# Repairs of the signal's ends in three sets of 4, 12 and 16 samples a layer, in place of eight of 4, in a four-layer convolution kernel

## The chip, the cores and the metric

The kernel runs on one core of one Trainium2 chip. Its engines are TensorE (PE; its weight load is listed apart as PEld), VectorE (DVE), ScalarE (ACT), GpSimd (POOL) and SyncE (SP), which issues most transfers. The metric is the device time of one execution in microseconds, lower is better. A profile is one execution, and its span runs from the first to the last instruction.

## The reference

The input `x` is 32 samples x 64 channels x 1024 positions. Four layers follow each other; each computes `x = x + ffn(cond(x, style))`, where `cond` is a chain of four modulated convolutions and `ffn` a layer of 1024 x 1024 with low-rank additions (another kind in each layer):

```python
TYPES = ('same', 'upsample', 'same', 'downsample')

def _layer(x, style, w, b, mw, mb, typ):
    s = style @ mw.T + mb
    weight = SCALE * w * s[:, None, :, None]
    demod = lax.rsqrt(jnp.sum(weight * weight, axis=(2, 3)) + EPS)
    weight = weight * demod[:, :, None, None]
...
x = x + _L0_ffn_ref(_L0_cond_ref(x, cond_512, ...), L0_ffn_A, L0_ffn_B, L0_ffn_Wr, L0_ffn_br)
x = x + _L1_ffn_ref(_L1_cond_ref(x, cond_512, ...), L1_ffn_gate, L1_ffn_kernel, ...)
x = x + _L2_ffn_ref(_L2_cond_ref(x, cond_512, ...), L2_ffn_base_W, L2_ffn_gate_W, ...)
x = x + _L3_ffn_ref(_L3_cond_ref(x, cond_512, ...), L3_ffn_W, L3_ffn_b, L3_ffn_A, ...)
```

The kernel composes the last three convolutions into one filter per sample. That composition is right inside the signal, but not at its first and last positions, where each single convolution pads with zeros. So the ends are computed again by the four convolutions one after the other, on the 8 positions at each side.

## The kernel before

**Steps.** Samples are worked on in 16 pairs per layer. A step is one pair; two steps (j = 0, the even one, and j = 1, the odd one) make one pass of a hardware loop `Fori` over `i`, and each engine runs its own such loop. Step n of a layer transposes and projects pair n, convolves pair n + 1 and prepares pair n + 2: `halves` and `filter` compose its filter, `first` applies the first convolution. Engines meet at semaphores only. `drain`, `enter` and `fill` are straight code between the loops of two layers; they also prepare the next layer's weights and modulations (`mods`), and end that with `mods_ready`.

**The repair of the ends.** It has five stages. Stage 0 (VectorE) scales the loaded ends into `e_x`. Stages 1 to 4 are one convolution each: three matmuls (six in stage 4) of plain fp32 on TensorE (`pe_edge`, L1055 and L1046), whose result VectorE scales, shifts and writes to `e_h`, `e_z`, a second tile that the profile also calls `e_z`, and `e_y` (`dve_edge`, L782 to L801). `end_hi` and `end_lo` take two values that `dve_first` copies into the convolution's input (L739, L740), and `dve_y` copies `e_y` into the result (L755). A set is four samples, so a layer has eight sets. Set 0 is repaired in `enter`, and set i + 1 in the even step of pass i, with the stages laid between the other matmuls of that step. TensorE waits for a stage where a bank of PSUM is used again:

```python
            if edges:

                pe.wait_ge(s["dve_e"], edge_count(l, i + 1, 4))
            if more:
                pe_halves(pe, l, n + 2)
            if edges:
                pe_edge(pe, l, i + 1, 2)
```

**The filter.** ScalarE and VectorE write a pair's filter to `filt`, and SyncE then shifts parts of it to other partitions by four transfers (L321, L322); the convolution (`pe_conv`) waits for them. In the odd steps of layer 0 SyncE also loads a block of the layer 1 kernel (`load_kernel`) ahead of the shift.

**Loads of the ends.** GpSimd issues them (`pool_load_edge`, L300 and L308). The tile `e_in` holds one set, and the next set is asked for when stage 0 has read it.

## Time and profile before

| what | before |
|---|---|
| median of 3 runs | 1951.31 us (1949.11 to 1953.24) |
| span of the profiled execution | 1944.8 us |
| TensorE busy | 1829.3 us, 94% |
| its weight loads | 1520.9 us, 78% |
| VectorE busy | 874.8 us, 45% |
| ScalarE busy | 667.7 us, 34% |
| GpSimd busy | 96.2 us, 5% |
| mean granted clock of TensorE | 0.966 |

The profile has no device time of its own execution, only the span, so the span stands beside the runs: it is 4.3 to 8.4 us below them. TensorE's busy time counts matmuls; weight loads run beside them.

### The profile page before, as it was taken

The page shows a single profiled execution, that of the slowest core. Times are in us where ns is not written, and L with a number is a line of the kernel's source. Part 1 is how long each engine was busy: PE and PEld are TensorE (multiplying, and loading weights), DVE is VectorE, ACT ScalarE, POOL GpSimd, SP SyncE. Part 2 cuts the span into 40 slices and gives each one's busy share as a digit, 9 for nine tenths or more (in the row PEclk, how much of TensorE's full clock was granted, in tenths as well). Part 3 has the DMA queues.
Part 4 walks back from the last instruction along what each step waited for, and adds up shares of the span by engine and source line. Part 5 has one row for each costly group of instructions (what it writes and reads, how often), then busy time and mean ns, then how long its engine had stood idle before and what let it go on. Part 6 is the DMA issues. An engine that isn't in the chain of part 4 may idle for free.

```text
span 1944.8 us, 28665 instructions
## 1 busy us (share of the span) xinstructions
PE 1829.3 (94%) x9728; PEld 1520.9 (78%) x9728; DVE 874.8 (45%) x2573; ACT 667.7 (34%) x1237; POOL 96.2 (5%) x173
## 2 busy tenths in 40 slices
PE   5889998979999999999899999999989999999995
PEld 4777787767888888887788888888767888888873
DVE  5155555644333333455543444444563333333327
ACT  2355555433333323325333222332253323332310
POOL 2000000010000000010000000000100000010000
PEclk9889999969999999999999999999999999999996
DMA  6565666436323322325322222221242222222218
GB/s 121 126 147 143 149 151 162 108 93 95 81 70 86 79 67 74 78 67 129 88 70 73 59 67 62 74 73 42 68 114 54 73 62 74 80 77 62 63 43 324
DMA packets 229831, 181.27 MB, mean 93 GB/s; under 512 B 178648, under 2 KB 189944, under 8 KB 229534
## 3 DMA queue, kind: packets, MB, share of 16 engines
q1 hardware_dynamic: 222142, 173.35, 34.7%
q10 hardware_dynamic: 2640, 5.26, 0.9%
q0 software_dynamic: 5008, 2.14, 0.9%
q8 instruction: 23, 0.38, 0.1%
q14 instruction: 18, 0.15, 0.0%
HBM read 108.34 MB, written 42.99 MB: 78 GB/s over the span
## 4 chain that ended last, share of the span: by engine, by line
PE 78%; issue 9%; DVE 4%; SPq 3%; DMA 3%; ACT 2%; POOL 0%; POOLq 0%; DVEq 0%; ACTq 0%
PE ps L970 64%; PE ps L1784 4%; PE ps L1055 3%; SPq L1321 3%; PE ps L1103 2%; DMA filt<-filt 2%; PE ps L1046 1%; ACT w_hi L1448 1%; PE ps L1804 1%; DVE x_last L1939 0%; POOL limes_rep L1864 0%; DVE filt L745 0%; DMA raw<-in_x 0%; PE ps L1996 0%; DMA raw<-in_L_ffn_base_W 0%
## 5 line engine op out<-in xcount | busy, mean ns | idle before, releaser
L970 PE MATMUL ps<-xp_hi,filt 128*128 128x512 f32 x1024 | 332.3, 406 | 13.5 <-DMA filt<-filt 12.0
L970 PE MATMUL ps<-w_hi,y_hi 128*128 128x512 f32 x768 | 314.1, 409 | 0.0
L970 PE MATMUL ps<-w_hi,y_lo 128*128 128x512 f32 x768 | 306.7, 399 | 0.0
L970 PE MATMUL ps<-w_lo,y_hi 128*128 128x512 f32 x768 | 305.8, 398 | 0.0
L970 PEld LDWEIGHTS ps<-xp_hi,filt 128*128 128x128 f32 x1024 | 187.2, 190 | 54.4 <-DMA filt<-filt 13.7
L734 DVE SCALAR_TENSOR_TENSOR xp_lo<-ps,mods_pair,xp_hi 128x512 fp32r<-128x512 f32 x128 | 96.2, 752 | 289.2 <-ACT xp_hi L403 289.1
L403 ACT ACTIVATE xp_hi<-ps,mods_pair 128x512 fp32r<-128x512 f32 x128 | 88.3, 690 | 379.9 <-PE ps L970 379.9
L970 PE MATMUL ps<-xp_lo,filt 128*128 128x512 f32 x512 | 202.5, 396 | 0.0
L970 PEld LDWEIGHTS ps<-w_lo,y_hi 128*128 128x128 f32 x768 | 146.2, 190 | 35.7
L419 ACT ACTIVATE y_nat<-ps,mods_pair 128x512 f32<-128x512 f32 x128 | 99.6, 778 | 215.3 <-PE ps L970 215.3
L970 PEld LDWEIGHTS ps<-w_hi,y_hi 128*128 128x128 f32 x768 | 147.3, 192 | 31.7
L970 PEld LDWEIGHTS ps<-w_hi,y_lo 128*128 128x128 f32 x768 | 146.6, 191 | 30.9
L428 ACT ACTIVATE y_hi<-ps 128x512 fp32r<-128x512 f32 x96 | 55.9, 599 | 324.2 <-PE ps L1103 324.2
L830 DVE TENSOR_TENSOR x_res<-ps,x_res 128x1024 f32<-128x1024 f32 x48 | 58.6, 1221 | 187.7 <-PE ps L970 187.7
L970 PE MATMUL ps<-x_hi,first_hi 128*128 128x512 f32 x256 | 109.3, 427 | 7.8 <-DVE w_lo L1452 5.9
L970 PEld LDWEIGHTS ps<-xp_lo,filt 128*128 128x128 f32 x512 | 97.4, 190 | 22.8
L755 DVE COPY y_nat<-e_y 128x4 f32<-128x4 f32 x128 | 21.8, 170 | 197.3 <-ACT y_nat L419 196.7
L308 POOL DMA_DIRECT2D e_in<-x_state x96 | 58.5, 616 | 1034.7 <-DVE e_x L782 994.5
L970 PE MATMUL ps<-x_lo,first_hi 128*128 128x512 f32 x256 | 104.3, 407 | 0.0
L970 PE MATMUL ps<-x_hi,first_lo 128*128 128x512 f32 x256 | 104.0, 406 | 0.0
L970 PE MATMUL ps<-fb_hi,up_hi 128*128 128x256 f32 x320 | 91.9, 287 | 0.0
L970 PE MATMUL ps<-fb_lo,up_hi 128*128 128x256 f32 x320 | 91.3, 285 | 0.0
(313 smaller groups left out, 3096.9 us busy)
## 6 DMA issues: line engine op xcount, KB each, us to landing
x_in<-x_state SPq DMA_DIRECT2D x96, 256.0 KB, 3.8
x_res<-x_state SPq DMA_DIRECT2D x48, 512.0 KB, 4.0
x_state<-x_res SPq DMA_DIRECT2D x46, 512.0 KB, 2.9
filt<-filt SPq DMA_DIRECT2D x128, 128.0 KB, 2.7
filt<-filt SPq DMA_DIRECT2D x128, 96.0 KB, 2.4
raw<-in_x SPq DMA_DIRECT2D x16, 512.0 KB, 4.9
x_res<-in_x SPq DMA_DIRECT2D x16, 512.0 KB, 4.0
x_state<-raw SPq DMA_DIRECT2D x16, 512.0 KB, 3.5
```

The source lines that it names most:

```text
L308: gp.dma_start(e_in[:, h, :, side, :], xs_edge[g, h, :, :, side * (M - 4):side * (M - 4) + 4]).then_inc(s["e_loaded"], 16)
L403: nc.scalar.activation(xp_hi[:, q, 1:M + 1], ps[:, 3 + 2 * q, :], ACT.Identity, bias=mods_pair[:, par, BX, q:q + 1]).then_inc(s["act_p"], 1)
L419: nc.scalar.activation(y_nat[q][:], ps[:, 6 + q, :], ACT.Identity, bias=mods_pair[:, par, CB, q:q + 1], scale=mods_pair[:, par, DS, q:q + ...
L428: nc.scalar.activation(y_hi[:, :, C * q:C * q + C], src, ACT.Copy).then_inc(s["act_t"], 1)
L734: nc.vector.scalar_tensor_tensor(xp_lo[:, q, 1:M + 1], ps[:, 3 + 2 * q, :], mods_pair[:, par, BX, q:q + 1], f(xp_hi[:, q, 1:M + 1]), ALU.a ...
L755: nc.vector.tensor_copy(ends, e_y[:, 2 * par + q]).then_inc(s["dve_y"], 1)
L830: nc.vector.tensor_tensor(dst.rearrange("p (h m) -> p h m", h=2), ps[:, 0:2, :], res, ALU.add).then_inc(s["dve_o"], 1)
L970: ins = nc.tensor.matmul(out, st[x0], mv[x1], start=first and t == 0, stop=last and t == 2, **kw)
L1055: last = mm(ps[0:rows, bank, 0:8 * width].rearrange("p (b e w) -> p b e w", b=4, e=2), st[k], rhs, start=k == 0, stop=k == 2)
L1103: last = nc.tensor.transpose(ps[:, 3 + 2 * q, P * t:P * t + P], y_nat[q][:, P * t:P * t + P], ident[:])
L1321: act.dma_start(dst, src).then_inc(s["small_loaded"], 16)
L1784: last = nc.tensor.matmul(ps[:, 0 if l == 0 else 6, 0:PROJ_W[l]], y_f[:, kb], proj[:, kb, 0:PROJ_W[l]], start=kb == 0, stop=kb == KB - 1)
```

## The change

The samples of a layer are repaired in three sets, which `EDGE_GROUPS` lists as first sample and count: 0 and 4, 4 and 12, 16 and 16. The first is still repaired on the way into the layer, the second in the even step of pass 0, the third in that of pass 3. These two passes are written out ahead of the loops over passes 1 to 2 and 4 to 6, on TensorE and VectorE only. Tiles of the repair hold 16 samples; `end_hi`, `end_lo` and `e_y` hold all 32, and are indexed by a register in the loops. The large tiles share memory with weights of the preparation, so their zero columns are written anew in each layer (four memsets ahead of `mods_ready`), and loads of the second and third set wait for `mods_ready`. The first set has a tile of its own, `e_first`. The diff, cut to its core:

```diff
 WIN = 4
 EDGE_OPS = 10
+EDGE_GROUPS = ((0, 4), (4, 12), (16, 16))
+EDGE_SETS = len(EDGE_GROUPS)
+EDGE_MOST = 16
+EDGE_STEPS = {0: 1, 3: 2}
...
         fb_hi, fb_lo = (sb(f"fb_{r}", [P, 2, WIN, C], F32R) for r in ("hi", "lo"))
+        with ExitStack() as area:
+
+            e_all = sb("e_all", [C, 2, EDGE_MOST, 2, 4], stack=area)
+            e_x = sb("e_x", [C, EDGE_MOST, 18], stack=area)
+            e_h = sb("e_h", [C, EDGE_MOST, 16], stack=area)
+            e_z = sb("e_z", [P, EDGE_MOST, 14], stack=area)
+            e_z2 = sb("e_z2", [P, EDGE_MOST, 12], stack=area)
...
-        e_y = sb("e_y", [P, 4, 2, 2])
+        e_first = sb("e_first", [C, 2, EDGE_GROUPS[0][1], 2, 4])
+        e_y = sb("e_y", [P, B, 2, 2])
+
+        def e_in(g):
+
+            return (e_first if g == 0 else e_all)[:, :, 0:EDGE_GROUPS[g][1]]
+
+        def e_in_nat(g):
+
+            n = EDGE_GROUPS[g][1]
+            t = (e_first if g == 0 else e_all)[:].rearrange("p a b e m -> p (a b e m)")
+            return t[:, 0:16 * n].rearrange("p (b e w) -> p b e w", b=n, e=2)
...
+            return EDGE_OPS * (EDGE_SETS * l + g) + step
+
+        def edge_set(k):
+
+            return sum(2 * k >= first for first, _ in EDGE_GROUPS) - 1
+
+        def edge_stage(l, g, stage_no):
+
+            return 4 * (EDGE_SETS * l + g) + stage_no
...
         def pool_load_edge(gp, l, g):
 
-            if not (l == 0 and is_zero(g)):
+            first, count = EDGE_GROUPS[g]
+            if g > 0:
+
+                gp.wait_ge(s["mods_ready"], l + 1)
+            if not (l == 0 and g == 0):
 
                 gp.wait_ge(s["dve_e"], edge_count(l, g - 1, 2))
             if l == 0:
                 for side in range(2):
-                    gp.dma_start(e_in_nat[:, :, side, :],
-                                 x_edge[g, :, :, side * (L - 8):side * (L - 8) + 8]).then_inc(s["e_loaded"], 16)
+                    gp.dma_start(e_in_nat(g)[:, :, side, :],
+                                 x_edge[:, first:first + count, side * (L - 8):side * (L - 8) + 8]).then_inc(s["e_loaded"], 16)
                 return
             for q in range(2):
 
-                gp.wait_ge(stored[q], 16 * (GROUPS * (l - 1) + g + 2))
+                gp.wait_ge(stored[q], 16 * (GROUPS * (l - 1) + (first + count) // 4 + 1))
             for h in range(2):
                 for side in range(2):
-                    gp.dma_start(e_in[:, h, :, side, :],
-                                 xs_edge[g, h, :, :, side * (M - 4):side * (M - 4) + 4]).then_inc(s["e_loaded"], 16)
+                    gp.dma_start(e_in(g)[:, h, :, side, :],
+                                 xs_edge[h, :, first:first + count, side * (M - 4):side * (M - 4) + 4]).then_inc(s["e_loaded"], 16)
...
+            for t, pad in ((e_x, 17), (e_h, 15), (e_z, 13), (e_z2, 11)):
+                v.memset(t[:, :, 0:pad + 1:pad], 0.0)
             v.memset(f(x_hi[:, :, 0:1]), 0.0)
             v.memset(f(x_lo[:, :, 0:1]), 0.0).then_inc(s["mods_ready"], 1)
...
-            b = 2 * par + q
-            nc.vector.tensor_copy(xp_hi[0:C, q, 1:M + 2:M], f(end_hi[:, b]))
-            nc.vector.tensor_copy(xp_lo[0:C, q, 1:M + 2:M], f(end_lo[:, b])).then_inc(s["dve_p"], 1)
+            b = ds(2 * k + q, 1)
+            nc.vector.tensor_copy(xp_hi[0:C, q:q + 1, 1:M + 2:M], f(end_hi[:, b]))
+            nc.vector.tensor_copy(xp_lo[0:C, q:q + 1, 1:M + 2:M], f(end_lo[:, b])).then_inc(s["dve_p"], 1)
...
-            nc.vector.tensor_copy(ends, e_y[:, 2 * par + q]).then_inc(s["dve_y"], 1)
+            nc.vector.tensor_copy(ends.unsqueeze(1), e_y[:, ds(2 * k + q, 1)]).then_inc(s["dve_y"], 1)
 
         def dve_edge(dve, l, g, stage_no):
 
             v = nc.vector
+            b0, n = EDGE_GROUPS[g]
 
             def mod(m, rows, width):
-                return mods[rows, m, ds(4 * g, 4)].unsqueeze(2).to_broadcast([rows.stop - rows.start, 4, width])
...
+                1: (2, lo_r, 14, e_h[:, 0:n, 1:15], G1, BT1),
+                2: (4, all_r, 12, e_z[:, 0:n, 1:13], G2, None),
+                3: (7, all_r, 10, e_z2[:, 0:n, 1:11], G3, BT3),
+                4: (7, all_r, 4, e_y[:, b0:b0 + n].rearrange("p b e m -> p b (e m)"), DS, None)}[stage_no]
+            dve.wait_ge(s["pe_e"], edge_stage(l, g, stage_no))
+            src = ps[rows, bank, 0:n * src_w].rearrange("p (b w) -> p b w", w=src_w)
             first = 2 * stage_no + 1
             done(v.tensor_tensor(dst, src, mod(mul, rows, src_w), ALU.mult), first)
             if stage_no == 1:
 
...
+        def dve_step(dve, l, i, j, more, one_more, g_next=None, g_y=None):
             n = 2 * i + j
-            edges = more and j == 0
-            g_y = i if j == 0 else i + 1
+            edges = g_next is not None
             if more:
                 dve_mods_pair(dve, l, n + 2, j)
             if edges:
-                dve_edge(dve, l, i + 1, 0)
+                dve_edge(dve, l, g_next, 0)
             if l > 0:
                 dve_y_lower(dve, l, n)
             if more:
...
         def pe_edge(pe, l, g, stage_no):
             mm = nc.tensor.matmul
 
+            n = EDGE_GROUPS[g][1]
             pe.wait_ge(s["dve_e"], edge_count(l, g, 2 * stage_no))
             if stage_no == 4:
                 for h in range(2):
                     for k in range(TAPS):
-                        rhs = e_z2[:].rearrange("p b (e w) -> p b e w", e=2)[:, :, :, k + h:k + h + 3:2]
-                        last = mm(ps[C * h:C * h + C, 7, 0:16].rearrange("p (b e w) -> p b e w", b=4, e=2),
+                        rhs = e_z2[:, 0:n].rearrange("p b (e w) -> p b e w", e=2)[:, :, :, k + h:k + h + 3:2]
+                        last = mm(ps[C * h:C * h + C, 7, 0:4 * n].rearrange("p (b e w) -> p b e w", b=n, e=2),
                                   down_T[:, k], rhs, start=k == 0, stop=k == 2)
...
-        def pe_step_0(pe, i, j, more, one_more):
+        def pe_step_0(pe, i, j, more, one_more, g_next):
             l, n = 0, 2 * i + j
-            edges = more and j == 0
+            edges = g_next is not None
             pe_transpose_y(pe, l, n, one_more)
             if one_more:
                 pe_conv(pe, l, n + 1, 0)
             if edges:
-                pe_edge(pe, l, i + 1, 1)
+                pe_edge(pe, l, g_next, 1)
 
             pe.wait_ge(s["act_f"], whole_y(l, n, 1))
...
-            for t in (e_x, e_h, e_z, e_z2):
-                gp.memset(t[:], 0.0)
             for t in (up_hi, up_lo, end_hi, end_lo):
                 gp.memset(f(t[:]), 0.0)
...
                 if l + 1 < LAYERS:
                     load_cond_weights(gp, l + 1)
-                with gp.Fori(0, GROUPS - 1) as i:
-                    pool_load_edge(gp, l, i + 1)
+                for g in range(1, EDGE_SETS):
...
-                with dve.Fori(0, GROUPS - 1) as i:
+                for i0, i1 in ((0, 3), (3, GROUPS - 1)):
                     for j in range(2):
-                        dve_step(dve, l, i, j, True, True)
+                        dve_step(dve, l, i0, j, True, True, EDGE_STEPS[i0] if j == 0 else None, edge_set(2 * i0 + j + 1))
+                    with dve.Fori(i0 + 1, i1) as i:
+                        for j in range(2):
+                            dve_step(dve, l, i, j, True, True, None, EDGE_STEPS[i0])
                 if l + 1 < LAYERS:
                     dve_drain(dve, l)
                 else:
...
-                with pe.Fori(0, GROUPS - 1) as i:
+                for i0, i1 in ((0, 3), (3, GROUPS - 1)):
                     for j in range(2):
-                        pe_step(pe, l, i, j, True, True)
+                        pe_step(pe, l, i0, j, True, True, EDGE_STEPS[i0] if j == 0 else None)
+                    with pe.Fori(i0 + 1, i1) as i:
+                        for j in range(2):
+                            pe_step(pe, l, i, j, True, True)
```

What stands where changes as follows, at the places that matter most. First TensorE in an even step of layer 1, in the loop, between the convolutions of the pair's two samples (`filt0`, `filt1`). Before:

```order
L970 MATMUL ps<-xp_hi,filt0 128x512 x2
L970 MATMUL ps<-xp_lo,filt0 128x512
L1041 ISA
L1055 MATMUL ps<-e_x,first_T 128x56 x3
L970 MATMUL ps<-xp_hi,filt1 128x512 x2
L970 MATMUL ps<-xp_lo,filt1 128x512
```

After, in the loop over passes 1 to 2 of that layer:

```order
L1000 MATMUL ps<-xp_hi,filt0 128x512 x2
L1000 MATMUL ps<-xp_lo,filt0 128x512
L1000 MATMUL ps<-xp_hi,filt1 128x512 x2
L1000 MATMUL ps<-xp_lo,filt1 128x512
L1000 MATMUL ps<-xp_hi,filt1 128x512 x2
```

Stage 1 and its wait (ISA) have left the looped steps, and so have the other stages. In the written-out even step of pass 3 they stand with sixteen samples, with 224 columns for 56:

```order
L1000 MATMUL ps<-xp_hi,filt0 128x512 x2
L1000 MATMUL ps<-xp_lo,filt0 128x512
L1086 MATMUL ps<-e_x,first_T 128x224 x3
L1000 MATMUL ps<-xp_hi,filt1 128x512 x2
L1000 MATMUL ps<-xp_lo,filt1 128x512
```

Second, VectorE at the end of a layer's preparation, where the last modulations are made. Before:

```order
L696 TENSOR_TENSOR mods<-ps,mods 128x32
L697 TENSOR_SCALAR mods<-mods,bias_col 128x32
L699 MEMSET x_hi 128x2
L700 MEMSET x_lo 128x2
L709 COPY mods_pair<-mods 128x20
```

After:

```order
L724 TENSOR_TENSOR mods<-ps,mods 128x32
L725 TENSOR_SCALAR mods<-mods,bias_col 128x32
L728 MEMSET e_x 64x16x2
L728 MEMSET e_h 64x16x2
L728 MEMSET e_z 128x16x2
L728 MEMSET e_z2 128x16x2
L729 MEMSET x_hi 128x2
L730 MEMSET x_lo 128x2
L739 COPY mods_pair<-mods 128x20
```

Four memsets have come in between the modulations and the last memset, which signals `mods_ready`.

## Rows read from the trace of the kernel before

**Rows 1.** The page: span, and busy time of each engine.

```profile
span 1944.8 us, 28665 instructions
...
PE 1829.3 (94%) x9728; PEld 1520.9 (78%) x9728; DVE 874.8 (45%) x2573; ACT 667.7 (34%) x1237; POOL 96.2 (5%) x173
```

**Rows 2.** Windows, odd then even step, layers 1 to 3: start:end length, busy (records), clock.

```profile
530.51:557.22 26.71, 26.71 (x137) 22.43 (x136) 9.06 (x22) 8.73 (x17) 0.00 (x0) 1.00 0.34 86
557.22:587.20 29.98, 29.98 (x168) 25.11 (x167) 12.54 (x37) 9.94 (x19) 2.45 (x4) 1.00 0.26 68
1031.11:1060.35 29.24, 29.24 (x153) 24.66 (x151) 12.17 (x38) 9.44 (x18) 0.00 (x0) 1.00 0.27 69
1060.35:1092.86 32.51, 32.51 (x183) 27.36 (x182) 14.51 (x51) 8.27 (x17) 2.43 (x4) 1.00 0.24 63
1491.83:1517.96 26.13, 26.13 (x134) 21.53 (x133) 9.16 (x23) 8.58 (x16) 0.00 (x0) 1.00 0.29 78
1517.96:1547.35 29.39, 29.39 (x163) 24.19 (x162) 11.42 (x36) 8.58 (x16) 2.44 (x4) 1.00 0.27 70
```

**Rows 3.** Windows of layer 0: five pairs of steps, and one odd step.

```profile
143.59:331.71 188.12, 175.87 (x1032) 146.52 (x1031) 107.80 (x315) 99.42 (x186) 6.12 (x10) 1.00 0.63 149
240.29:256.58 16.29, 15.77 (x89) 13.42 (x89) 9.65 (x25) 10.56 (x19) 0.00 (x0) 1.00 0.59 151
```

**Rows 4.** Waits of TensorE in those five pairs: us in total, times, longest.

```profile
PE ps L970 <- DMA filt<-filt: 9.6, 5, 2.4
PE ps L970 <- DVE zt_lo L1767: 2.6, 5, 0.5
```

**Rows 5.** Groups by line and shape, TensorE's fp32 matmuls: records, busy us, mean ns.

```profile
L1784 PE MATMUL ps<-proj,y_f 128*128 128x136 f32 x256 | 35.0, 292 | 0.7 <-ACT y_f L430 0.7
...
L1055 PE MATMUL ps<-e_x,first_T 64*128 64x56 f32 x192 | 29.8, 291 | 6.5 <-DVE e_x L777 5.2 <-DVE e_x L782 1.3
L1055 PE MATMUL ps<-e_h,up_st 64*128 64x48 f32 x192 | 29.0, 286 | 0.0
...
L1055 PE MATMUL ps<-e_z,mid_T 128*128 128x40 f32 x192 | 25.6, 276 | 0.0
...
L1046 PE MATMUL ps<-e_z,down_T 128*64 128x16 f32 x384 | 21.7, 214 | 0.0
```

**Rows 6.** Timeline of an even step of layer 0: start us, us, engine.

```profile
226.66 0.21 DVE L797 TENSOR_TENSOR e_h<-e_h,mods 64x56 f32<-64x56 f32 x1
...
227.29 0.75 DVE L728 SCALAR_TENSOR_TENSOR x_lo<-raw,mods_pair,x_hi 128x512 fp32r<-128x512 f32 x1
...
227.59 0.43 PE L970 MATMUL ps<-gu_hi,mid_hi 128*128 128x384 f32 x1
```

**Rows 7.** The way from layer 0 to 1: timeline, and TensorE's wait there.

```profile
401.29 0.06 DVE L699 MEMSET x_hi<- 128x2 f32 x1
...
PE ps L1055 <- DVE e_x L782: 1.3, 1, 1.3
```

**Rows 8.** First step of layer 2: its window, and TensorE's waits in it.

```profile
935.84:969.37 33.53, 32.79 (x181) 27.39 (x182) 14.41 (x53) 9.82 (x19) 2.43 (x4) 1.00 0.27 76
...
PE ps L1103 <- DVE xp_lo L740: 1.3, 2, 0.7
```

**Rows 9.** The shift in layer 0: timeline and transfer, even step; the chain, odd step.

```profile
236.56 0.63 SPq L322 DMA_DIRECT2D filt<-filt  x1
...
filt<-filt SPq DMA_DIRECT2D x1, 128.0 KB, 2.7
...
240.28 0.85 PEld L1103 LDWEIGHTS ps<-ident,y_nat 128*128 128x128 f32 x8 [0.44 <-DVE e_y L801]
...
253.77 5.60 DMA filt<-filt
```

**Rows 10.** The page, transfers of instructions: queue, packets, MB, share of 16 engines.

```profile
q8 instruction: 23, 0.38, 0.1%
```

**Rows 11.** Window of another even step of layer 3; the last numbers are clock, DMA, GB/s.

```profile
1629.01:1659.95 30.94, 30.94 (x163) 25.35 (x163) 11.43 (x36) 8.57 (x16) 2.44 (x4) 0.94 0.26 66
```

More of the change, by code:

```diff
@@ L156, in build @@
         xp_lo = sb("xp_lo", [P, 2, M + 4], F32R)
-        end_f = sb("end_f", [C, 4])
-        end_hi, end_lo = (sb(f"end_{r}", [C, 4, 2], F32R) for r in ("hi", "lo"))
+        end_f = sb("end_f", [C, EDGE_MOST])
+        end_hi, end_lo = (sb(f"end_{r}", [C, B, 2], F32R) for r in ("hi", "lo"))
         filt = [sb(f"filt{q}", [P, WIN, 2, 2, C], F32R) for q in range(2)]
@@ L780, in dve_edge @@
                 for h in range(2):
[L781 to L782 removed]
+                    dst = e_x[:, 0:n, 1:17].rearrange("p b (e m h) -> p b e m h", e=2, h=2)[:, :, :, :, h]
+                    done(v.tensor_tensor(dst, e_in(g)[:, h], m, ALU.mult), h + 1, False)
                 return
             bank, rows, src_w, dst, mul, add = {
[L785 to L790 removed]
+                1: (2, lo_r, 14, e_h[:, 0:n, 1:15], G1, BT1),
[4 more added lines that the diff above has]
+            src = ps[rows, bank, 0:n * src_w].rearrange("p (b w) -> p b w", w=src_w)
             first = 2 * stage_no + 1
@@ L798, in dve_edge @@
             elif stage_no == 2:
-                done(v.tensor_tensor(dst, dst, up_bias[:, ds(4 * g, 4), :], ALU.add), first + 1)
+                done(v.tensor_tensor(dst, dst, up_bias[:, b0:b0 + n, :], ALU.add), first + 1)
             else:
@@ L1142, in pe_step_0, with pe_step @@
             if edges:
-                pe_edge(pe, l, i + 1, 4)
+                pe_edge(pe, l, g_next, 4)
             pe_tail(pe, l, i, j)
             if edges:
-                pe.wait_ge(s["dve_e"], edge_count(l, i + 1, EDGE_OPS))
-        def pe_step(pe, l, i, j, more, one_more):
+                pe.wait_ge(s["dve_e"], edge_count(l, g_next, EDGE_OPS))
+        def pe_step(pe, l, i, j, more, one_more, g_next=None):
             if l == 0:
-                pe_step_0(pe, i, j, more, one_more)
+                pe_step_0(pe, i, j, more, one_more, g_next)
                 return
             n = 2 * i + j
-            edges = more and j == 0
+            edges = g_next is not None
             pe_transpose_y(pe, l, n, one_more)
```

86 lines of the change are left out of this document (36 added, 50 removed).

## The prediction

> **What bounds the kernel now.** I read the profile's page first. TensorE is busy for 1829.3 of the 1944.8 us span, every other engine for less than half (PEld is its own weight load) [rows 1]. What counts is therefore TensorE's own work, and the few places where it waits. Then I cut the trace into steps. A step begins with the transposes of `y_nat` (L1103); even steps (j = 0) carry a set of end repairs, odd ones don't. In layers 1 to 3 TensorE is busy for the whole of both kinds: 26.71 of 26.71 us without a set and 29.98 of 29.98 us with one in layer 1, and so on [rows 2]. No wait lies in either. The two kinds differ by 29.98 - 26.71 = 3.27, 32.51 - 29.24 = 3.27 and 29.39 - 26.13 = 3.26 us. The counts show what it is: 168 against 137 matmul records, and one set issues 15 matmuls of plain fp32, which leave two records each, 30 in all. So a set costs TensorE 3.26 us, whatever it holds, and VectorE's part in it is hidden.
>
> Layer 0 is different. Five pairs of steps take 188.12 us, 37.62 each; the odd one is 16.3 us, so the even one is 21.3 us [rows 3]. In those five pairs TensorE waits 9.6 us for the `filt` shift, 1.9 us per even step, always at its start [rows 4]. An even step without that wait is 19.4 us, and a set costs 19.4 - 16.3 = 3.1 us there.
>
> **The change, part by part.** Before, 7 even steps of each layer carry a set, and the way into a layer carries one. After, 2 even steps do (of 12 and 16 samples), and the way in is as it was.
>
> *Sets removed.* Five per layer. Layers 1 to 3: 15 x 3.26 = 48.9 us. Layer 0: 5 x 3.1 = 15.5 us, if the even step then looks like the odd one. Together 64.4 us.
>
> *Sets made wider.* Eight sets stay in steps; four grow to 12 and four to 16 samples. The columns of one matmul grow from 56, 48, 40 and 16 to 224, 192, 160 and 64 for 16 samples. I read what one more record costs as (busy time / number of sets - mean of one) / (records - 1): e_x (29.8/32 - 0.291)/5 = 0.128 us, e_h 0.124, e_z 0.105, e_y (21.7/32 - 0.214)/11 = 0.042. The fp32 projection of layer 0, with 136 columns and 16 records a step, gives (35.0/16 - 0.292)/15 = 0.126 us [rows 5]. 56 and 136 columns cost the same, so up to there the price is fixed, and 0.126/136 = 0.93 ns per column is a ceiling for fp32. By the ceiling 224, 192, 160 and 64 columns take 0.208, 0.179, 0.149 and 0.059 us, and a set of 16 grows by 6 x 0.080 + 6 x 0.055 + 6 x 0.044 + 12 x 0.017 = 1.3 us; a set of 12 (168, 144, 120, 48 columns) by 6 x 0.028 + 6 x 0.010 + 6 x 0.007 + 12 x 0.003 = 0.3 us. The four layers give 6.4 us. The floor is 0, since the trace shows no slope between 56 and 136 columns. The widest row is the nearest to the new widths, and it bounds from above; I take 5 us.
>
> The Trainium skill ("FP8 and Floating Point Precision", TensorE Precision Notes) says that true fp32 makes four passes through the array. With two records per matmul that would be two passes in one record, an estimated 0.83 ns per column at 2.4 GHz, and the eight sets would grow by some 4 us. The trace agrees as far as it goes: 136 columns would need 0.113 of the 0.126 us.
>
> *VectorE's part.* Its operations grow too. Between 56 and 512 elements the time goes from 0.21 to 0.75 us, 1.2 ns per element, so each of the two e_h operations of a set of 16 takes 0.2 us more. The tightest cover is in layer 0: the second e_h operation ends at 226.87 and TensorE reaches `halves`, which waits for it, at 227.59 [rows 6]. That is 0.7 us of slack against 0.4 us more. In layers 1 to 3 a whole convolution of 12 matmuls lies there. What isn't covered is the last pair of operations, e_y in layer 0, for which TensorE stands already [rows 9]: under 0.1 us in each of the two steps, 0.2 us in all, and 0.1 us for a wider e_x in the layer's first step.
>
> *Four memsets in the preparation.* They stand ahead of `mods_ready` on VectorE, 0.06 us each by the two that are there. Only on the way from layer 0 to 1 does TensorE wait for this chain (1.3 us) [rows 7]; elsewhere it has work or stands behind loads. 0.3 us.
>
> *Loads.* The set of 16 is asked for when the set of 12 has been read, which is three pairs of steps before it is needed (over 100 us in any layer). The set of 12 is asked for at `mods_ready`, behind the same wait as the load in its place before. I cost them at nothing; what hides them is the rest of the way into the layer. If the cover were gone TensorE would stand before its first e_x.
>
> *Written-out steps and registers.* VectorE gets a register operation for `end_hi` and `e_y` in the loops; it idles half the time. TensorE gets two loop entries per layer for one. The back edges cost nothing today (the windows of rows 2 that begin a pass are fully busy). The first step of layer 2, which enters the loop, is 33.53 us, 1.0 us over the later even ones, but the trace gives that to two waits for `xp_lo`, 1.3 us, which belong to the way in [rows 8]. I cost entries at 0.
>
> **The shift in layer 0.** This is where the saved time could come back. In an even step the last shift of sample 0 is issued at 236.56 and lands 2.7 us later, at 239.26; the transposes ahead of the convolution that needs it end at 241.13 [rows 9]. Slack 1.9 us. Behind `pe_filter` stand e_z (6 x 0.105 = 0.6 us), e_y (12 x 0.042 = 0.5) and the wait for e_y (0.4); without them the convolution would be due at 239.6, and 0.5 us later if the short wait for `zt_lo` of the odd steps [rows 4] turns up, as I expect. So it is just covered, with 0.8 us left over. In the odd step the same shift takes 5.60 us [rows 9], since it shares the queues with the kernel's block, and the even step has no such load.
>
> **Sum.** -64.4 + 5.0 + 0.3 + 0.3 = -58.8 us. The profiled execution's span 1944.8 becomes 1886.0. The median of the runs, 1951.31, lies 6.5 us over the span (what stands around the first and last instruction, and the spread of the runs), so the time is 1951.3 - 58.8 = 1892.5 us, rounded to 1893, 3.0% less. By the ends of the column price it is 1887.5 to 1894.
>
> **Rivals.**
> 1. *The shift becomes the limit of layer 0's even steps too.* Removing 3 us brings transfers closer (the DMA engines are already 63% busy there [rows 3]). If the shift takes 5.6 us as in the odd step, the even step pays 2.9 us more less the 0.8 us left over, 5 x 2.1 = 10.5 us in all: 1903 us. For it: the odd steps; against it: the even step issues no kernel block.
> 2. *Branches and code.* Each layer gets a second loop entry and leaves a loop twice. At 1 us each (the excess of rows 8, should it not be `xp_lo` after all) 4 entries and 4 exits are 8 us: 1901 us. The Trainium skill ("Runtime: NRT & Kernel Launch", Instruction fetch mechanics) says that a taken branch outside the fetched blocks stalls for a transfer, while straight code is fetched ahead in blocks of 16 KiB. By the second half the written-out steps would be free. No back edge shows the first half here.
> 3. *Slower.* TensorE's code grows from 1881 to 4369 rows. The instruction queue q8, by its size TensorE's, fetched 23 blocks [rows 10]; in that proportion there would be 30 more. If each held TensorE up, the gain of 58.8 us would be gone from 2.0 us per block on; at 3 us the time would be 1893 + 90 = 1983 us. Against it: the fetches of before leave no wait in the windows of the first passes beyond those explained.
> 4. *The clock.* One even step of layer 3 is 30.94 us with a granted clock of 0.94 instead of 29.39 [rows 11], 1.55 us for one such dip. Denser work might bring more: five more are 8 us, 1901 us. It might also lose the two of before, -3 us.
>
> **How the numbers follow.** Forecast (1886 to 1896, with the runs' spread of 2 us either way): 0.66. Rival 1, wholly or in part: 0.13. Rival 2: 0.06. Rival 3: 0.03. Rival 4: 0.07. A larger gain (the shift's wait shrinks with the even step, down to 1884): 0.05. The range 1886 to 1903 leaves out rival 3, what lies past the full price of 1, and a little below. A measurement of this kernel tells about 0.2% from no change. Faster 0.96, same 0.01, slower 0.03.
>
> **What would show it.** In the changed profile: even steps without a set equal to odd ones, 26.7, 29.2 and 26.1 us in layers 1 to 3, and 18 to 18.5 in layer 0; the steps with 16 samples about 1 us over 29.98, 32.51 and 29.39; e_x records with 224 columns 0.19 us apart; 360 fp32 records of the repairs for 960; the wait for the `filt` shift near 10 us and only behind odd steps; no wait for e_x in the first steps of layers 1 to 3. Waits of TensorE at loop entries, or for `filt` behind even steps, would make it wrong.

## The result

The median fell from 1952.28 us (4 runs, 1949.11 to 1955.01) to 1906.2 us (4 runs, 1902.64 to 1909.07): a ratio of 0.9758, with a 95% interval of 0.9737 to 0.9778. That is 46.1 us less, where I had forecast 58.8 us less, and above the top of the range, 1903. The profiled execution took 1907.9 us, with a span of 1906.1.

The page of the changed kernel answers to [rows 1, 10]:

```profile
span 1906.1 us, 25849 instructions
...
PE 1778.4 (93%) x9128; PEld 1476.4 (77%) x9128; DVE 839.0 (44%) x2329; ACT 665.4 (35%) x1237; POOL 58.1 (3%) x99
...
q8 instruction: 49, 0.80, 0.2%
```

There are 600 fewer records on TensorE, 20 sets of 30, as the change says. The span shrank by only 38.7 us between these two profiles. So I cut the trace into steps again. Stretches of layers 1, 2 and 3 first (columns as in [rows 2]): for each layer an even step without a set, and the step that carries 16 samples.

```profile
505.90:532.75 26.85, 26.85 (x137) 22.42 (x136) 10.42 (x24) 9.84 (x19) 0.00 (x0) 1.00 0.29 77
...
613.11:644.43 31.32, 31.32 (x168) 25.96 (x166) 13.56 (x37) 9.95 (x19) 0.00 (x0) 1.00 0.25 66
...
986.38:1015.61 29.23, 29.23 (x152) 24.66 (x151) 12.25 (x38) 8.14 (x17) 0.00 (x0) 1.00 0.25 70
1103.30:1137.13 33.83, 33.83 (x182) 28.16 (x181) 15.59 (x51) 8.26 (x17) 0.00 (x0) 1.00 0.22 61
...
1497.40:1523.50 26.10, 26.10 (x133) 21.51 (x132) 9.24 (x23) 8.57 (x16) 0.00 (x0) 1.00 0.29 78
1601.83:1632.53 30.70, 30.70 (x163) 25.01 (x162) 12.49 (x36) 8.58 (x16) 0.00 (x0) 1.00 0.25 67
```

Here the forecast holds to a tenth: 29.98 became 26.85, 32.51 became 29.23, 29.39 became 26.10, and the sets of 16 cost 1.3 us more than the old ones (31.32, 33.83, 30.70). Now layer 0: five pairs of steps, then single even steps, of which the third carries 16 samples. The number behind the busy times is the granted clock.

```profile
145.29:331.71 186.42, 168.56 (x911) 140.25 (x910) 100.58 (x263) 99.47 (x186) 0.00 (x0) 0.97 0.66 152
```

```profile
145.29:164.55 19.26, 15.97 (x89) 13.35 (x88) 9.73 (x25) 9.29 (x19) 0.00 (x0) 1.00 0.74 165
...
181.30:201.52 20.22, 17.53 (x89) 14.49 (x88) 9.72 (x25) 9.32 (x18) 0.00 (x0) 0.92 0.67 151
...
218.08:242.50 24.42, 21.98 (x119) 17.73 (x118) 13.06 (x38) 9.28 (x18) 0.00 (x0) 0.93 0.58 136
...
331.71:354.68 22.97, 18.68 (x89) 15.52 (x88) 9.75 (x25) 9.30 (x18) 0.00 (x0) 0.85 0.63 136
```

Layer 0 gained next to nothing: 188.12 us [rows 3] became 186.42, although four sets are gone from these ten steps. Two things took their place. TensorE's waits in the same window:

```profile
PE ps L1000 <- DMA filt<-filt: 11.8, 5, 2.6
PE ps L1000 <- DVE zt_lo L1798: 5.9, 9, 0.7
```

The first is the wait for the filter's shift, the second one for `zt_lo`, an operand that VectorE writes. They make 17.7 us for the 12.2 us of [rows 4]. And the clock: the same 89 records take 15.97 us at a mean clock of 1.00, 17.53 at 0.92 and 18.68 at 0.85. A mean under 1 comes from stretches in which the granted clock is 0.5, that is 1.2 GHz instead of 2.4; the texts below call them windows at 0.5 or at half clock, or dips. The kernel before had none in this loop:

```profile
143.59:369.59 226.00, 211.04 (x1238) 175.82 (x1237) 129.51 (x378) 118.02 (x222) 10.39 (x17) 1.00 0.61 146
```

### The profile page after: what moved, and what is told of

Its sections match the earlier page's. It is cut to its first block, busy times and chain, and to the rows that moved or that the text cites. A ratio compares the mean times of both kernels' runs of the same rounds, so it can differ in the third digit from the quotient of the medians.

```text
span 1906.1 us, 25849 instructions
## 1 busy us (share of the span) xinstructions
PE 1778.4 (93%) x9128; PEld 1476.4 (77%) x9128; DVE 839.0 (44%) x2329; ACT 665.4 (35%) x1237; POOL 58.1 (3%) x99
## 4 chain that ended last, share of the span: by engine, by line
PE 63%; issue 23%; DVE 5%; SPq 3%; DMA 3%; ACT 2%; POOL 1%; POOLq 0%; DVEq 0%; ACTq 0%
PE ps L1000 54%; PE ps L1815 3%; SPq L1352 3%; DMA filt<-filt 2%; PE ps L1134 2%; PE ps L1086 1%; DVE w_lo L1483 1%; DMA raw<-in_L_ffn_W 1%; DVE x_last L1970 1%; DVE filt L775 0%; POOL limes_rep L1895 0%; PE ps L2027 0%; ACT w_hi L1479 0%; ACT filt L441 0%; PE ps L1835 0%
## 5 line engine op out<-in xcount | busy, mean ns | idle before, releaser
L1000 PE MATMUL ps<-xp_hi,filt 128*128 128x512 f32 x1024 | 336.2, 410 | 18.0 <-DMA filt<-filt 15.8
L1000 PEld LDWEIGHTS ps<-xp_hi,filt 128*128 128x128 f32 x1024 | 192.5, 194 | 62.7 <-DMA filt<-filt 15.2
L785 DVE COPY y_nat<-e_y 128x4 f32 (+1 forms) x128 | 21.8, 170 | 222.5 <-ACT y_nat L447 221.9
L1000 PE MATMUL ps<-fb_hi,up_lo 128*128 128x256 f32 x320 | 90.3, 282 | 0.0
```

The costliest lines, as they stand in the source:

```text
L785: nc.vector.tensor_copy(ends.unsqueeze(1), e_y[:, ds(2 * k + q, 1)]).then_inc(s["dve_y"], 1)
L1000: ins = nc.tensor.matmul(out, st[x0], mv[x1], start=first and t == 0, stop=last and t == 2, **kw)
```

## The experiments

All ratios are against the kernel before, run on the same chip at the same time. "Loop of layer 0" is the stretch of its steps 2 to 13, with TensorE's busy time in it.

| kernel | median us | ratio (95% interval) | loop of layer 0 | busy | clock there |
|---|---|---|---|---|---|
| before | 1952.28 | 1 | 226.00 | 211.04 | 1.00 |
| before, second profile | 1951.11 (1 run) | | 225.93 | 211.02 | 1.00 |
| changed | 1906.2 | 0.9758 (0.9737 to 0.9778) | 225.84 | 203.02 | 0.96 |
| changed, second profile | 1904.02 (1 run) | | 221.38 | 201.55 | 0.97 |
| layer 0 with eight sets | 1912.8 | 0.9783 (0.9763 to 0.9804) | 231.01 | 214.13 | 0.99 |
| eight sets, code written out | 1959.58 | 1.0036 (1.0018 to 1.0055) | 232.70 | 214.04 | 0.99 |
| shift first | 1887.26 | 0.9659 (0.9637 to 0.9682) | 204.70 | 195.89 | 1.00 |
| shift first, again | 1887.76 | 0.9657 (0.9626 to 0.9688) | 204.61 | 195.61 | 1.00 |
| before, with shift first | 1939.29 | 0.9919 (0.9892 to 0.9946) | 213.91 | 210.61 | 1.00 |
| filled wait | 1899.1 | 0.972 (0.9689 to 0.9752) | 218.13 | 208.08 | 0.99 |
| before, ends by register | 1953.96 | 1.0013 (0.9995 to 1.0031) | 225.00 | 210.81 | 1.00 |
| shift first, unused tile | 1882.22 | 0.9638 (0.9608 to 0.9668) | 207.07 | 196.08 | 1.00 |
| two sets, shift first | 1868.11 | 0.9557 (0.953 to 0.9584) | 197.69 | 189.65 | 1.00 |

### The kernel before, a second profile

> The kernel before, unchanged, for a second profile. Theory 1 (its first profile was a low one): the span now is 1947 to 1951 with a mean clock of 0.955 to 0.965, and layer 0 or the way from layer to layer shows stretches at half clock that the first did not have. Theory 2 (such stretches come with the change alone): the span is within 1 us of 1944.8, the clock 0.966, and layer 0 from 115 to 390 us has no window at 0.5.

Theory 1 in its span: 1949.4 us, 4.6 more than the first. But layer 0 was as in the first, 225.93 for 226.00 us in its loop and no window at half clock. In that point theory 2 was right. The first profile had just been a low one, and so part of the gap between the 38.7 us of the spans and the 46.1 us of the medians is no miss.

### The changed kernel, a second profile

> The changed kernel again, for a second profile. Theory 1 (the windows at half clock in layer 0 belong to the kernel's own idle waits): three or more of them again between 180 and 391 us, the wait for the shifted filter 14.5 to 16.5 us in 6, layer 0 within 2 us of 345.6. Theory 2 (they were an accident of one execution): none or one, layer 0 at 336 to 340. The wait for the feed-forward weights on the way from layer 2 to 3, 3.5 us where the kernel before had 1.2, is read again too.

Theory 1 on the clock: windows at 0.5 began at 150.6, 222.3, 263.2 and 334.9 us. Layer 0 as a whole took 339.73 us, which is in the range of theory 2, and the waits were lower than theory 1 said: in the stretch from 146.02 to 330.62 us, and then two even steps without a set, one at full clock and one not:

```profile
PE ps L1000 <- DMA filt<-filt: 10.3, 5, 2.3
...
183.08:201.48 18.40, 15.98 (x90) 13.36 (x89) 9.72 (x25) 9.29 (x18) 0.00 (x0) 1.00 0.71 163
...
258.44:278.94 20.50, 17.55 (x90) 14.71 (x89) 9.81 (x25) 9.33 (x19) 0.00 (x0) 0.92 0.69 155
```

An even step without a set is 18.4 or 18.5 us where the clock stays up and 20.4 to 20.5 where it does not: 1.55 us more of work and the rest more of waiting. The span was 1902.2 us, 47.2 less than the kernel before's second.

### Layer 0 with its eight sets

```diff
+EIGHT = (0,)
+SETS = [GROUPS if l in EIGHT else EDGE_SETS for l in range(LAYERS)]
-            return EDGE_OPS * (EDGE_SETS * l + g) + step
+            return EDGE_OPS * (sum(SETS[:l]) + g) + step
...
+            if l not in SPLIT:
+                with eng.Fori(0, GROUPS - 1) as i:
+                    yield False, i
+                return
```

> The new form with layer 0 as it was: eight sets of 4 samples in one loop; layers 1 to 3 keep their three sets. Theory 1 (in layer 0 the change gains nothing, since the waits for the shifted filter and for zt_lo and the lower clock take back what the sets free): within 3 us of the changed kernel's 1906. Theory 2 (layer 0 did gain the 13 to 15 us of its term, and the miss is in the other layers): 1916 to 1922. In either case steps 0 to 13 of layer 0 are read again, 21.0 to 21.8 us the even and 16.3 the odd, and the wait for the shifted filter is near 12 us in 6.

1912.8 us lies between the two theories: by the ratios the three sets gain some 5 us in layer 0 (0.9783 against 0.9758), with intervals that overlap. Its loop of layer 0 is no copy of the one before, though: 231.01 us for 226.00, with two windows at half clock. So it bounds the gain from above. An even step with such a window, and the waits in the layer:

```profile
182.16:205.23 23.07, 20.93 (x120) 16.91 (x118) 12.02 (x38) 9.29 (x18) 1.22 (x2) 0.93 0.60 140
...
PE ps L1015 <- DMA filt<-filt: 11.4, 6, 2.0
```

The step has all its work, with a set of 4 samples in it, and its waits are no longer than those of [rows 4]. The clock fell all the same.

### Eight sets in the written-out code

```diff
+EIGHT = (0, 1, 2, 3)
+SPLIT = (0, 1, 2, 3)
...
+            for i0, i1 in ((0, 3), (3, GROUPS - 1)):
+                yield True, i0
+                with eng.Fori(i0 + 1, i1) as i:
+                    yield False, i
```

> The sets of before, eight of 4 samples in every layer, in the code of the change: passes 0 and 3 written out, two loops a layer. It prices the branches and the 26 more blocks of code by themselves. Theory 1 (they cost nothing that PE sees): 1950 to 1955, as before. Theory 2 (the rival of branches and code, 8 us): 1958 to 1963. Theory 3 (a fetch of 2 us or more for each block): over 2000.

1959.58 us is in the range of theory 2: 0.36% or 5.6 us over the 1953.94 us of the kernel before on the same chip. Where the time lies speaks against its cause. Its page and stretches: the blocks of code, then an even and an odd step of layer 1, then an even one of layer 0.

```profile
q8 instruction: 51, 0.84, 0.2%
...
504.21:534.21 30.00, 30.00 (x168) 25.09 (x167) 12.65 (x37) 9.93 (x19) 2.44 (x4) 1.00 0.27 70
534.21:560.96 26.75, 26.75 (x138) 22.44 (x136) 9.14 (x22) 8.73 (x17) 0.00 (x0) 1.00 0.33 86
...
178.71:202.24 23.53, 20.94 (x120) 16.83 (x118) 12.02 (x38) 9.18 (x18) 1.22 (x2) 0.93 0.64 140
```

28 more blocks than before leave the steps of layer 1 as they were, 29.98 and 26.71 [rows 2], so neither blocks nor branches hold TensorE in layers 1 to 3. 5.0 us of the loss lie in layer 0 (348.34 us for 343.36), where two of the even steps, 23.53 and 23.82 us long, fell into a stretch at half clock.

### The shift ahead of the kernel's block

```diff
+            if more:
+                sp_shift_filter(sp, l, n + 2)
             if l == 0 and load_next and j == 1:
                 load_kernel(sp, i + 2)
-            if more:
-                sp_shift_filter(sp, l, n + 2)
```

> The new form with one issue moved: in the odd steps of layer 0 SyncE sends the four filter shifts before the two loads of the next kernel block. Theory 1 (the shift is late because the block's 512 KB lie in front of it): the wait for the shifted filter falls from 15.5 us to under 8, and the time to 1895 to 1902. Theory 2 (the shift is late from its own landing and from the write of the filter, the block is only a bystander): the wait stays at 14 to 16 us and the time within 2 us of 1906. Theory 3 (the block now lands late and its split holds ScalarE): a new wait on the kernel's halves, 1908 to 1915.

1887.26 us: theory 1, and more of it than it gave. SyncE's timeline in an odd step of layer 0 of the changed kernel, and under it the transfers issued from 255 to 262 us (the last number is us to landing):

```profile
251.10 1.47 SPq L313 DMA_DIRECT2D raw<-in_x  x2
252.88 0.96 SPq L1411 DMA_DIRECT2D x_in<-in_L_ffn_kernel  x2
255.23 0.64 SPq L349 DMA_DIRECT2D filt<-filt  x1
255.92 0.62 SPq L350 DMA_DIRECT2D filt<-filt  x1
256.65 1.73 SPq L349 DMA_DIRECT2D filt<-filt  x1
...
filt<-filt SPq DMA_DIRECT2D x2, 128.0 KB, 5.6
filt<-filt SPq DMA_DIRECT2D x2, 96.0 KB, 6.1
```

The same with the shift first, issues from 242 to 250 us:

```profile
242.64 0.62 SPq L349 DMA_DIRECT2D filt<-filt  x1
243.31 0.62 SPq L350 DMA_DIRECT2D filt<-filt  x1
244.04 0.59 SPq L349 DMA_DIRECT2D filt<-filt  x1
244.68 0.63 SPq L350 DMA_DIRECT2D filt<-filt  x1
245.60 0.97 SPq L1411 DMA_DIRECT2D x_in<-in_L_ffn_kernel  x2
...
filt<-filt SPq DMA_DIRECT2D x2, 128.0 KB, 3.8
filt<-filt SPq DMA_DIRECT2D x2, 96.0 KB, 3.8
```

The shift lands in 3.8 us instead of 5.6 and 6.1, and its third issue takes 0.59 us instead of 1.73. The Trainium skill ("DMA: Bandwidth & Descriptors", Queues, rings and completion order) says that each DMA engine takes the descriptors of one queue in the order of the ring; by that rule the shift stands behind the block's 512 KB, and the trace agrees, with the 5.6 and 6.1 us behind the block and 3.8 us ahead of it. TensorE's waits in the loop, and the stretches of an even step, of the one with 16 samples and of the loop:

```profile
PE ps L1000 <- DVE zt_lo L1798: 7.3, 11, 0.7
PE ps L1000 <- DMA filt<-filt: 1.4, 5, 0.4
...
175.31:192.19 16.88, 15.98 (x90) 13.37 (x89) 9.75 (x25) 9.31 (x18) 0.00 (x0) 1.00 0.82 183
...
209.03:229.89 20.86, 20.46 (x120) 16.78 (x119) 13.07 (x38) 9.29 (x18) 0.00 (x0) 1.00 0.68 160
141.51:346.21 204.70, 195.89 (x1088) 163.78 (x1086) 120.19 (x313) 118.09 (x222) 4.29 (x7) 1.00 0.70 162
```

The wait for the shifted filter is all but gone, and so is every stretch at half clock in the loop: 14 us of idle time and 7.1 us of busy time less than in the first profile of the changed kernel. A second run with the same kernel:

> The changed kernel with the shift first once more, on the chip and with the runs of before of the one with the unused tile, as the measure of it. Theory: 0.966 of the kernel before again, 1885 to 1890, the wait for the shifted filter under 2 us and no window at 0.5 between 115 and 350 us.

It came out so: 0.9657, 1887.76 us, a wait of 1.5 us in 5, no window at half clock in the loop.

### The same move in the kernel before

> The kernel before with the same one move: in the odd steps of layer 0 the four filter shifts are issued ahead of the next kernel block's two loads. Theory 1 (the shift's chain bounded the even steps of layer 0 before too, by its 11.8 us in 6 waits, and the sets ran partly in its shadow): the even steps fall from 21.0 to 21.6 to 19.7 to 20.2, the time to 1940 to 1946; the three sets are then worth 1887 less that, 53 to 59 us, which is the whole sum. Theory 2 (in the kernel before the block load was no bound, and the move pays only with the three sets): the time stays at 1951 to 1955.

Theory 1 in its cause: 1939.29 us, 16 us less than before on the same chip (0.9919), and even steps of 19.2 to 19.5 us, both a little under its ranges. An even step that carries a set, and the loop:

```profile
179.05:198.22 19.17, 19.17 (x120) 15.89 (x118) 11.90 (x38) 9.33 (x19) 1.22 (x2) 1.00 0.72 169
...
143.38:357.29 213.91, 210.61 (x1237) 175.84 (x1236) 129.57 (x378) 118.05 (x222) 10.36 (x17) 1.00 0.64 154
```

With the shift out of the way, 0.9659 / 0.9919 = 0.974 is what the three sets do, 51 us of 1952, and not the 53 to 59 of theory 1. That it is more than the 46 us in the order that the change left is within the intervals of the ratios; the traces show it better. The sets shorten the loop of layer 0 by 9.2 us here (213.91 to 204.70), and by 0.2 and 4.5 us there (226.00 to 225.84, 225.93 to 221.38). The five even steps that lose their set fall from 19.17-19.45 to 16.71-17.08 us, 2.5 us each and not 3.1, and the odd steps grow from 16.3 to 16.6 on average. In both kinds stands the wait for `zt_lo`: 7.3 us in 11 waits, where the kernel before has 3.2 in 6 with the same move.

### The wait filled with work

```diff
             pe.wait_ge(s["dve_p"], smp(l, k, q))
+            for _ in range(8 if fill and q == 0 else 0):
+                nc.tensor.matmul(ps[:, 6, :], xp_hi[:, 0, 0:P], xp_hi[:, 0, 0:M], start=True, stop=True)
             pe.wait_ge(filt_shifted[q], 32 * (pid(l, k) + 1))
```

> The changed kernel as it was given, without the move, with eight multiplications of 128 x 512 on TensorE ahead of the wait for the shifted filter in the even steps of layer 0, into the bank that the next multiplication starts afresh; the output does not change. Theory 1 (the granted clock in layer 0 falls because TensorE stands idle for 2.0 to 3.6 us at that wait): the five windows at 0.5 between 185 and 391 us are gone, the wait shrinks by about 1.8 us each, no step is longer, and the time is 1896 to 1900. Theory 2 (the clock falls for another reason, and the idle wait is a bystander): as many windows at 0.5, time 1904 to 1909. Theory 3 (the filling is on the path): over 1910.

1899.1 us: theory 1, but for one step. Waits, the step with 16 samples and an even step without a set in layer 0:

```profile
PE ps L1000 <- DMA filt<-filt: 2.8, 4, 1.9
...
212.65:238.36 25.71, 23.85 (x128) 19.13 (x126) 13.06 (x38) 9.29 (x18) 0.00 (x0) 0.93 0.57 130
254.59:273.14 18.55, 17.85 (x97) 14.77 (x96) 9.73 (x25) 9.32 (x19) 0.00 (x0) 1.00 0.73 165
```

One window at 0.5 was left in the loop, where the changed kernel had four in either profile. It is in the step with 16 samples, the only one in which TensorE still stood idle for over 1 us at a stretch (1.86 us, and the clock fell after it); that step grew from 24.1-24.4 to 25.71 us, against the words "no step is longer". The five even steps without a set took 18.45 to 18.91 us, so work that does nothing made the kernel faster, by 3 to 8 us in that loop. The intervals of the two ratios just overlap (0.9720 and 0.9758), so the median alone would not show it; the traces do. The Trainium skill ("TensorE: Matmul & The Clock Gate", HAM oscillation) tells of a kernel whose clock falls again and again while TensorE waits for transfers. The trace agrees in part: of the eight windows in the loop in the changed kernel's two profiles seven began 0.1 to 1.5 us behind an idle stretch of 2.0 to 2.4 us, and one within a stretch of 3.6 us, but stretches of 1.8 to 2.6 us also passed without one.

### The ends by register

```diff
-            b = 2 * par + q
-            nc.vector.tensor_copy(xp_hi[0:C, q, 1:M + 2:M], f(end_hi[:, b]))
+            b = ds(2 * k + q, 1)
+            nc.vector.tensor_copy(xp_hi[0:C, q:q + 1, 1:M + 2:M], f(end_hi[:, b]))
...
-            nc.vector.tensor_copy(ends, e_y[:, 2 * par + q])
+            nc.vector.tensor_copy(ends.unsqueeze(1), e_y[:, ds(2 * k + q, 1)])
```

> The kernel before with one part of the change alone: the repaired ends of all 32 samples are kept, and VectorE's three copies of a sample's ends are addressed by a register instead of by a fixed place. Sets, loops and issues are as before. The two kernels with eight sets and the changed copies had odd steps of layer 0 of 16.44 us where the kernel before has 16.31, a wait for zt_lo of 0.67 us for 0.53, and two or three windows at 0.5 in layer 0. Theory 1 (the register makes VectorE late by 0.13 us a step in layer 0, and that also brings the lower clock there): odd steps 16.44, zt_lo 0.67, one to three windows at 0.5 between 140 and 371 us, 1954 to 1962 us. Theory 2 (it comes from the wider tiles of the sets or from the written-out code): 16.31, 0.53, none, and 1951 to 1956.

Half of theory 1: the steps and the wait, not the clock. An odd step of layer 0, and the wait for `zt_lo` in the layer:

```profile
165.17:181.63 16.46, 15.78 (x88) 13.40 (x89) 9.73 (x25) 10.56 (x19) 0.00 (x0) 1.00 0.59 153
...
PE ps L970 <- DVE zt_lo L1767: 4.7, 7, 0.7
```

The register, with the wider tiles that it needs (`end_hi`, `end_lo` and `e_y` hold 32 samples), costs each odd step 0.15 us (16.46 for 16.31). It brings no window at half clock, the loop is 1 us shorter than before (225.00), since the waits for the filter fell to 8.6 us in 6, and the time is the same within the interval. What makes the loop of layer 0 5 to 7 us longer in the two kernels with eight sets in the new form is therefore not this alone, nor the branches, since one of the two has none of its own in layer 0. The wider tiles of the sets and the order of the loads were not taken apart.

### Two sets, and a tile that nobody uses

```diff
-EDGE_GROUPS = ((0, 4), (4, 12), (16, 16))
-EDGE_MOST = 16
-EDGE_STEPS = {0: 1, 3: 2}
+EDGE_GROUPS = ((0, 8), (8, 24))
+EDGE_MOST = 24
+EDGE_STEPS = {0: 1}
...
+        room = sb("room", [P, 160])
```

The kernel with two sets has the unused tile too, and more that the cut leaves out: `e_all` shares memory with `e_z`, so VectorE writes the zero columns of both `e_z` tiles anew in stage 1, and the load of the second set waits for the first set's last stage.

> The new form with the shift first, and two sets a layer, of 8 and 24 samples, the second in step 0 of the layer; one loop in place of two. The waits of a set measured 3.15 us in all with 4 samples, 3.7 with 12 and 4.6 with 16. Theory 1 (from 12 to 16 they grow by 0.84 us for 4 samples, and go on so): 6.2 for 24 and 3.4 for 8, 1.7 us less a layer than with 4, 12 and 16: 1878 to 1883. Theory 2 (a set's waits are nearly the same at any width): 3.7 us less a layer, 1871 to 1874. Theory 3 (the set of 24 is late at its loads, or its chain on VectorE holds the rest of step 0): 1887 or more.

> The changed kernel with the shift first and an unused tile of 640 bytes a partition behind wsq_T, so that x_hi and everything after it lies where it does in the kernel with two sets; the work is the same as with the shift first. In that kernel every step without a set was 0.10 to 0.20 us shorter (26.74 and 26.58, 29.23 and 29.02, 26.11 and 25.97). Theory 1 (this comes from where the tiles lie): the same short steps here, 42 steps of layers 1 to 3 by some 0.15 make 6 us less than with the shift first. Theory 2 (it comes from the single loop in place of two, or from the missing set): the steps are 26.74, 29.23 and 26.11 as before, and the time that of the shift first within 2 us.

Two sets take 1868.11 us, below all three expectations, and are the fastest kernel of this study. Stretches: the first step of layer 2 with 24 samples, and a later one.

```profile
889.77:926.81 37.04, 35.65 (x182) 28.85 (x181) 16.38 (x55) 10.22 (x19) 0.00 (x0) 1.00 0.20 66
...
984.96:1013.98 29.02, 29.02 (x152) 24.67 (x151) 12.25 (x38) 9.45 (x18) 0.00 (x0) 1.00 0.23 71
```

The set of 24 costs 37.04 - 34.55 = 2.5 us more than the set of 12 in the same step with the shift first; the set of 16 saves 4.4 to 4.7 us in layers 1 to 3 and 4.0 in layer 0 by being gone. Four layers of some 2.2 us make 9 of the 19 us. Part of the rest is the second row: 29.02 us for 29.23, the same records. The kernel that only has the unused tile shows it too:

```profile
997.06:1026.15 29.09, 29.09 (x152) 24.69 (x151) 12.26 (x38) 9.45 (x18) 0.00 (x0) 1.00 0.23 71
```

All 13 steps behind the first in each of layers 1 to 3 became 0.10 to 0.21 us shorter by moving tiles 640 bytes on, so theory 1 holds in the steps, 6 us over the kernel. The medians say 5.5 us (1887.76 and 1882.22), with intervals that overlap, and the spans do not show it (1883.5 us, for 1880.8 and 1886.0 with the shift first): the loop of layer 0 was 2.4 us longer, 207.07 us, and its cause is open. The last 4 us between the two sets and the three I cannot assign; 3 of them are in the loop of layer 0, 197.69 us where 204.70 less the 4.0 would be 200.7.

## Why the prediction was wrong

**What held.** Sets removed in layers 1 to 3: 3.1, 3.28 and 3.29 us per step for the 3.26 forecast. Code and branches at nothing there. No wait for the filter behind even steps of layer 0; it stayed behind odd ones, as forecast. Layers 1 to 3 together, from the first transposes of layer 1 to the last step of layer 3, went from 1433.8 to 1390.9 us in the first profiles and from 1436.9 to 1392.8 in the second: 42.9 and 44.1 us less, where my terms make 45.

**The step that failed: "Layer 0: 5 x 3.1 = 15.5 us, if the even step then looks like the odd one".** Layer 0 went from 343.36 to 345.55 us and in the second profiles from 343.40 to 339.73, so 2.2 more and 3.7 less, where my terms make 14 less. Of the 11.6 us between the forecast 58.8 and the 47.2 of the second profiles, 10 lie here. The five even steps that lost their set took 106.3 us before, and 102.0 and 98.3 after, where the forecast makes 90.8. Of the 11.2 and 7.5 us too many, 5.8 and 4.7 are busy time above 15.97 us a step, which is the clock, and 5.4 and 2.8 are idle time. Three things are in the place of the step that failed:

- *The clock.* I had given it a rival of 0.07, five dips of 1.55 us, for the reason that "denser work might bring more". The size was nearly right: four windows in the loop in either profile, three of them in these five steps and one in the step with 16 samples, at 1.55 us of busy time each (17.53 - 15.98) and 2.7 for the one of double length. The reason was the opposite: in layer 0 the clock fell at idle time. That the idle wait brings it is shown from two sides: with the wait removed (shift first) no window is left, and with it filled only the one behind the wait that stayed. That a wait became harmful because a set's work is missing beside it is not shown. 18.40 - 15.98 = 2.4 to 19.26 - 15.97 = 3.3 us of idle time do stand beside 16 us of work now, where it was some 2 beside 19.4. But the two kernels with eight sets in the new form have 19.4 us of work beside waits of 1.8 to 2.6 us, and the clock fell in 4 of their 12 even steps; in the kernel before, with waits of 1.6 to 2.4, in none of 12. What decides which wait is followed by the lower clock stays open.
- *The wait for the shift.* I kept its 9.6 us as a constant. It was 11.8 and 10.3 us in the same ten steps. It was no constant of the layer but a matter of order on SyncE: 1.4 us with the four issues moved. I had noted that the odd step's shift takes 5.60 us since it shares the queues with the block, and had drawn no consequence but for the even step.
- *The wait for zt_lo.* I had put 0.5 us of it into the slack of the shift and left it out of the sum. It now stands in both kinds of step, 5.9 us for 2.6 in ten steps, and 0.15 us of each is the register addressing with its tiles, which I had costed at nothing. With the shift out of the way it is what is left of the miss: the sets then shorten layer 0 by 9.5 us (332.00 to 322.48), where my terms make 14.

**A size too small: "I take 5 us" for the wider sets.** The first stage's records before and after, in a step of layer 3, and the group of the latter:

```profile
1521.78 0.87 PE L1055 MATMUL ps<-e_x,first_T 64*128 64x56 f32 x6
...
1605.63 1.40 PE L1086 MATMUL ps<-e_x,first_T 64*128 64x224 f32 x6
...
L1086 PE MATMUL ps<-e_x,first_T 64*128 64x224 f32 x6 | 1.4, 366 | 0.0
```

The steps with 16 samples grew by 1.31 to 1.34 us in layers 1 to 3, as the ceiling of 0.93 ns a column gave it (1.3), and by more than 2 in layer 0, with one dip in it. But the ceiling's two parts were both off. In the trace, records of 224, 192 and 160 columns start 0.189, 0.163 and 0.136 us apart, as the prediction's signs said (0.19), which is 0.84 to 0.85 ns a column and next to its other estimate, 0.83. What makes up for that is the other end: records of 56 columns start 0.112 us apart and not 0.128, and the first record of the stage takes 0.294 us for 0.154 up to the next. My formula, (busy - mean) / (records - 1), spreads the first one's time over all.

**The profile and the median.** I summed against the first profile's span and added 6.5 us to come to the median. The second profile of the kernel before had 4.6 us more, so most of those 6.5 us were this profile's luck. The terms were differences of steps, so this did not bend the sum; it made the first comparison of spans look 8 us worse than it was.

**The rivals.** Rival 1, the shift as the limit of even steps too, did not happen: no wait for the filter stands behind an even step. A time of its size was lost, but to the clock and to the waits that had been there. Rivals 2 and 3 are out in layers 1 to 3: in their loops no step at full clock got longer by more than 0.04 us with 28 more blocks of code. (Of the 1.0 us that [rows 8] shows over the later steps, only 0.7 is idle time, 33.53 - 32.79; the wait of 1.3 us that I named for it lies partly ahead of that step.) In layer 0 5 us of the size of rival 2 remain with the code written out, most of them in two steps at half clock, and at no branch that I could name. Rival 4 also held that the two dips of before might go, 3 us less, and they did: layer 3 has two even steps of 30.94 us in both profiles of before, in which TensorE is busy throughout, and none in either profile of the changed kernel. So the 42.9 and 44.1 us of layers 1 to 3 hold these 3 us, against 2.7 and 3.5 us lost on the way from layer 2 to layer 3; and a dip can also come without an idle wait.

**What stays open.** On the way from layer 2 to layer 3 TensorE waits for the feed-forward weights, before and after the change:

```profile
PE ps L1547 <- DMA raw<-in_L_ffn_W: 1.2, 1, 1.2
```

```profile
PE ps L1578 <- DMA raw<-in_L_ffn_W: 4.0, 2, 3.5
```

The last step of layer 2, with that way in it, is 62.2 to 62.4 us in the two profiles of before and 64.2 to 67.4 in all eleven others, the kernel before with the shift first (65.16) and the one with the ends by register (65.49) among them. Two things go with it in the traces: in that step the clock is at 0.5 for 10.2 us in those two profiles and for 13.7 to 20.5 in the others, and TensorE is idle for 8.8 us and for 9.3 to 12.4. The four loads are issued 40 to 46 us into the step in both kernels, but the third and fourth land after 5.3 and 7.0 us before the change and after 9.6 and 9.7 behind it. Why they land later I do not know, and no experiment was made for it.

## What to carry to other kernels

When work is taken out of a step that waits for a transfer, price the idle time that is left, and look whether the clock falls behind it: then part of the saving comes back as slower work. Ask which other waits the work had covered. Look at what the issuing queue sends ahead of the transfer that is waited for, and whether that has to be in front; here four issues moved past two gave 19 us. And read a price per column from the distance of record starts, not from a mean over a group that includes its first record.

## What the runs showed of the hardware

- In the loop of layer 0 the granted clock fell to 0.5 only at idle stretches of TensorE: eight times in two profiles of the changed kernel, with 2.0 to 3.6 us idle. Stretches of 1.8 to 2.6 us in the same kernel, and all twelve of 1.6 to 2.4 us in the kernel before, passed without it. In two steps of layer 3 of the kernel before it fell with no idle time at all (30.94 us for 29.39).
- Eight multiplications whose result is thrown away, put ahead of the wait for the filter in each even step, left the length of the steps at full clock as it was (18.45 to 18.91 us against 18.40 to 19.26) and kept the granted clock at 1.00 in all five steps without a set. The step with 16 samples kept a wait and a mean clock of 0.93.
- Plain fp32 multiplications leave two records each. Those of 160 to 224 columns start 0.84 to 0.85 ns a column apart (0.189 us for 224), and those of 56 columns 0.112 us apart.
- A shift of the tiles by 640 bytes a partition made the steps of layers 1 to 3 behind the first shorter by 0.4 to 0.7% (26.74 to 26.55, 29.23 to 29.09, 26.11 to 25.97 us), with the same records. Which operand's place matters was not taken apart.
- The same shift of 128 KB within on-chip memory landed after 3.8 us ahead of a 512 KB load on its queue and after 5.6 us behind it, and the third issue behind the load took 1.73 us for 0.59.
